# Grouped-query cross-attention layers: all value products of a tile moved behind the tile's last row-maximum products

## What is computed

```python
# 16 query heads, 4 key and value heads, head width 32, n_rep = 4
xn = rmsnorm(x, norm_w)
q = (xn @ wq).reshape(B, T, N_HEADS, HEAD_DIM)
k = (cond @ wk).reshape(B, S, N_KV_HEADS, HEAD_DIM)
v = (cond @ wv).reshape(B, S, N_KV_HEADS, HEAD_DIM)
qg = q.reshape(B, T, N_KV_HEADS, n_rep, HEAD_DIM)
scores = jnp.einsum('btgrd,bsgd->bgrts', qg, k) * scale
attn = jax.nn.softmax(scores, axis=-1)
out = jnp.einsum('bgrts,bsgd->btgrd', attn, v).reshape(B, T, N_HEADS * HEAD_DIM)
return x + out @ wo
```

## Time and profile before

| | |
|---|---|
| Time, median of 3 runs | 4637.84 us (4637.76 to 4638.88) |
| The profiled execution: time | 4637.64 us |
| its span, first to last instruction | 4635.9 us |
| mean granted TensorE clock | 0.976 of full speed |
| PE busy | 4336.0 us, 94% |
| DVE busy | 2565.3 us, 55% |
| ACT busy | 1986.6 us, 43% |
| POOL busy | 1809.3 us, 39% |
| a1's loop, by the repeated pattern | about 2471 to 4620 us of the span |

### The profile page before, as it was taken

How to read it: one execution, slowest core, us unless ns; L and a number is a source line. 1 busy time by engine, 2 the same in 40 slices (tenths; PEclk the granted TensorE clock), 3 DMA queues, 4 the chain that set the end, 5 groups by cost and what they waited for, 6 DMA issues and landing times. The chain is left out here.

```text
span 4635.9 us, 63591 instructions
## 1 busy us (share of the span) xinstructions
PE 4336.0 (94%) x20066; PEld 2694.6 (58%) x20066; DVE 2565.3 (55%) x3575; ACT 1986.6 (43%) x2444; POOL 1809.3 (39%) x923
## 2 busy tenths in 40 slices
PE   7999799996999999999978999999999998999998
PEld 6888588883556555655644554544554554455454
DVE  2122200014555455545447777787777777777776
ACT  2111211112333333333325566566656656666665
POOL 0000000002353444344434556555555555555655
PEclk9999899997999999999988999999999999999999
DMA  4333422224444444444442223322322322232233
GB/s 155 130 127 131 155 80 82 79 88 131 107 115 115 109 102 120 115 109 113 107 125 62 81 73 90 88 83 81 92 81 75 94 84 86 82 88 79 77 95 97
DMA packets 301729, 461.95 MB, mean 100 GB/s; under 512 B 44955, under 2 KB 95131, under 8 KB 301693
## 3 DMA queue, kind: packets, MB, share of 16 engines
q1 hardware_dynamic: 301692, 461.50, 34.4%
HBM read 227.88 MB, written 102.76 MB: 71 GB/s over the span
## 5 line engine op out<-in xcount | busy, mean ns | idle before, releaser
L813 DVE TENSOR_REDUCE a_max_cols<-a_ps 128x1 f32<-128x512 f32 x2072 | 1323.4, 677 | 329.4 <-PE a_ps L937 327.0
L707 ACT ACTIVATE a_probs<-a_ps 128x1024 f32<-128x1024 f32 x1024 | 1018.6, 1027 | 735.8 <-PE a_ps L958 732.7
L937 PE MATMUL a_ps<-a_k_ops,a_q_ops 96*128 96x512 f32 (+1 forms) x2592 | 955.0, 433 | 42.7 <-DVE a_max_cols L813 30.9
L937 PEld LDWEIGHTS a_ps<-a_k_ops,a_q_ops 96*128 96x128 f32 (+1 forms) x2592 | 459.8, 190 | 627.0 <-DVE a_max_cols L813 490.9
L958 PE MATMUL a_ps<-a_q_ops,a_k_ops 128*128 128x512 f32 x2560 | 780.0, 407 | 36.3 <-ACT a_probs L707 20.7
L595 POOL TENSOR_TENSOR a_probs<-a_probs 128x1024 f32<-128x1024 f32 x192 | 463.3, 2413 | 726.9 <-PE a_ps L974 705.7
L974 PE MATMUL a_ps<-a_probs,a_v 128*32 128x512 f32 (+1 forms) x4096 | 674.6, 610 | 0.0
L958 PEld LDWEIGHTS a_ps<-a_q_ops,a_k_ops 128*128 128x128 f32 x2560 | 462.5, 190 | 215.7 <-ACT a_probs L707 104.4
L595 POOL TENSOR_TENSOR a_sums<-a_probs 128x1024 f32<-128x1024 f32 x192 | 454.3, 2385 | 5.0 <-ACT a_probs L707 5.0
L595 POOL TENSOR_TENSOR a_sums<-a_sums,a_probs 128x1024 f32<-128x1024 f32 x192 | 455.2, 2390 | 0.3
L601 POOL TENSOR_TENSOR a_qn_lo<-a_qf,a_qn_hi 128x512 fp32r<-128x512 f32 x99 | 126.7, 1280 | 791.2 <-ACT a_qn_hi L662 791.2
(11 more groups left out here) (92 smaller groups left out, 5615.5 us busy)
## 6 DMA issues: line engine op xcount, KB each, us to landing
a_k_ops<-k_scratch SPq DMA_DIRECT2D x201, 256.0 KB, 4.0
a_q_ops<-a_qn_hi SPq DMA_DIRECT2D x792, 64.0 KB, 2.0
k_scratch<-kp_out SPq DMA_DIRECT2D x88, 512.0 KB, 2.8
a_q_ops<-a_qn_hi SPq DMA_DIRECT2D x268, 128.0 KB, 2.3
a_x_raw<-out_t SPq DMA_DIRECT2D x26, 1024.0 KB, 5.3
a_q_ops<-a_qn_lo SPq DMA_DIRECT2D x396, 64.0 KB, 2.0
a_x_res<-out_t SPq DMA_DIRECT2D x96, 256.0 KB, 3.1
out_t<-a_results SPq DMA_DIRECT2D x96, 256.0 KB, 2.0
```

What stands on the lines that cost most here:

```text
L707: act.activation(probs[:, s], ps[:, 2 * (s % 2):2 * (s % 2) + 2, :], ACT.Exp)\
L813: dve.tensor_reduce(max_cols[:, col:col + 1], bank(MAXB[n]), AX.X, ALU.max, negate=True).then_inc(reduced, 1)
L937: last = pe.matmul(bank(MAXB[n]), q_ops[0:rows(p), s, h, p, q * P:(q + 1) * P], k_ops[0:rows(p), s, k_head(h), p, :], start=(p == 0), stop ...
```

## The change

Only PE's order in a1 is changed. The four output groups leave the loop over r and stand behind it, directly ahead of the denominators, so that six groups of the same form follow one another. The wait for `ms_step`, which in t0 stood ahead of the first output group, moves with it into `outputs`. For a0 the new table gives the same order as before. No instruction is added or removed.

```diff
-    OUT_AT = (2, 3, 5, NS - 1) if has_norm else (1, 2, 3)
+
+    OUT_AT = {} if has_norm else {1: (0,), 2: (1,), 3: (2,)}
+    OUT_LAST = [kt for kt in range(KT) if not any(kt in kts for kts in OUT_AT.values())]
...
                     pe.wait_ge(normed, 1 + it * T + t)
+                    if has_norm and t == 0:
+                        pe.wait_ge(ms_step, MS * (it + 1) + 1)
...
                     for r in range(NS):
-                        if has_norm and r == NS - 1:
-                            outputs(it, t, KT - 1)
...
-                        if r in OUT_AT and not (r == NS - 1 and has_norm):
-                            if has_norm and t == 0 and r == OUT_AT[0]:
-                                pe.wait_ge(ms_step, MS * (it + 1) + 1)
-                            outputs(it, t, OUT_AT.index(r))
-                    if not has_norm:
-                        outputs(it, t, KT - 1)
-                    else:
+                        for kt in OUT_AT.get(r, ()):
+                            outputs(it, t, kt)
+                    for kt in OUT_LAST:
+                        outputs(it, t, kt)
+                    if has_norm:
                         denominators(it, t)
```

## The result

The changed kernel takes 4807.85 us (median of 4 runs, 4804.99 to 4811.39) against 4638.11 us before (4 runs, 4637.76 to 4638.88): ratio 1.0366, 95% interval 1.0348 to 1.0384, slower by 170 us. The forecast of 4790 us was 18 us low and the sign was right. The changed kernel's profiled execution took 4811.39 us, with a span of 4809.6 us.

A forecast was written before the change was run, and what follows sets the result against it. It took DVE to set the pace in the loop over r and PE, in line with ACT, the other half. 4637.6 us + 142 for four tiles over 24 iterations + 11 for weight splits = 4790 us, range 4735 to 4850.

The forecast's parts named there:

- The mechanism: Output groups lie in PE time covered by DVE's reductions; moved behind the loop, four cost 3.56 us uncovered per tile.
- three signs of being wrong: Maxima closer than 0.61 us, t0 growing by less than 3 us, or a granted clock in the loop not 1.00.
- The order alone: Sum over four tiles: t0 3.4, t1 0.55, t2 1.17, t3 0.80, so 5.9 us per iteration, 142 us.
- the line of groups: Behind the last maxima: entered after 0.55 us, then four groups at 0.89 us each before the denominators.
- the last maxima: In t0 they stay where they are, the first output group takes the denominators' place, and t0 grows 3.4 us.
- The clock: First rival: it falls in t0's thin loop, 43 us over 24 tiles, 4833; all 96 tiles 4960; beyond t0 0.13.
- the likeliest case: The main case, chance 0.70: 142 us from the four tiles plus 11 us from weight-splitting tiles, 4790 us.
- The x split in t1: DVE splits x under the output groups, projection only 0.4 us later; exposed table load delays t2: t1 +0.55, t2 +0.3.
- The weight-splitting tiles: In three t1 and three t0, two of four groups run at half clock: 1.8 us each, 11 us.
- The groups in the loop cost nothing at all: In t0 DVE never pauses, so moving the groups out of the loop frees nothing there.
- the second rival: PE is the bound and its switches delay DVE; each group saves 0.31 us, 119 us in all, 4519 us; chance 0.05.

The follow-up runs named there:

- dup_t0_old: The order of before in all tiles, with the first output group of t0 issued twice: 4654.05 us, ratio 1.0034.
- only_t23: The changed kernel with t0 and t1 back in the order of before, so only t2 and t3 have the new one: 4658.62 us, ratio 1.0039.
- warm_mid: The changed kernel with six extra matmuls in every tile, each pair ahead of the second maximum of r = 5, 6, 7: 4803.73 us, ratio 1.0360.
- dup_t3_last: The changed kernel with the first output group of t3 issued twice, behind the loop: 4819.78 us, ratio 1.0390.
- only_t0: The changed kernel with t1, t2 and t3 back in the order of before, so t0 alone has the new one: 4758.16 us, ratio 1.0252.
- t1_old: The changed kernel with t1 back in the order of before: 4773.99 us, ratio 1.0283.
- warm_t1: The changed kernel with six extra matmuls in t1, two behind the maxima of each of r = 5, 6 and 7: 4812.53 us, ratio 1.0365.
- only_t0_warm: only_t0 with six extra matmuls in t0, two behind the maxima of each of r = 5, 6 and 7: 4722.43 us, ratio 1.0188.

## Why the prediction was right, and where its terms were off

The mechanism was right: groups that lay beside DVE's reductions now stand in the open, and DVE waits for the denominators instead. That the time came out within 18 us is in part luck: two errors of opposite sign met. Of the forecast's own three signs of being wrong, one came outright: the granted clock in the loop was not 1.00 but 0.85 over t1. One came by a hair, since the maxima ran every 0.60 us and not every 0.61. The third stayed away narrowly: t0 grew by 3.05 us, and less than 3 would have been the sign.

1. **The order alone was over-sized.** Tiles of the changed kernel with no fall of the clock: t0 22.48 (+3.05, forecast 3.4), t1 20.53 in nine iterations (+0.26, forecast 0.55), t2 19.55 (+0.94, forecast 1.17), t3 30.59 (+0.42, forecast 0.80). Together 4.67 us per iteration, 112 us, where I had 5.92 and 142. The four values come from different iterations; no run had the whole new order free of falls. In t2 and t3 the step at fault is the line of groups: entered after 0.43 us, not the 0.55 taken from the earlier trace rows, with groups of 0.865, not 0.89, and reductions every (8.45 - 0.63) / 13 = 0.60 us instead of 0.61. Over four groups and eleven reductions that makes 0.12 + 0.10 + 0.11 = 0.33 us. In t0 the last maxima, which I took to stay where they were, let the groups begin 13.93 us into the tile, where the denominators had begun 14.16 us into it (3740.78 - 3726.85 against 3381.00 - 3366.84). With the 0.10 of the groups and 0.03 of the two behind them this is 0.36 us, the gap between 3.4 and 3.05.
2. **The clock was a rival and should have been in the sum.** I gave it to t0 alone, 0 to 43 us, and kept it out of the likeliest case since no gap comes near 2 us. No iteration of the changed kernel is free of it. In 12 it falls in a t1 without a weight split, where it makes 23.01 of 20.53 (2.48 us), and in seven in such a t0 (24.2 us once, else 25.0 to 25.2, of 22.48). In the tiles without a weight split that adds up to 46 us. In place of a long idle gap the traces show waits for a maximum's bank of 0.8 to 0.9 us in t0, and in t1 one wait of 1.18 us for ACT. The Trainium skill (TensorE: Matmul & The Clock Gate, Why this matters for your kernels) warns of long idle gaps between bursts; the clock fell here without one, and measurement decides.
3. **The x split in t1.** It was right that the late split no longer holds the projection of q (the wait of 1.42 us is gone) and that the table load passes on to t2. In the iteration shown the load ends at 3677.92 and the first exponential of t2 starts at 3677.93, 1.22 us behind the tile's first score product, where that was 0.65 us before. With t1 in its old order t2 is 0.46 us shorter (I had 0.3).
4. **The weight-splitting tiles.** The 11 us that I added for them did come. The six tiles concerned grew by 13 us more than the order alone gives. The largest is the t1 that went from 25.4 to 29.9 us, its granted clock from 0.93 to 0.77. By length alone this is hard to see, since nearly every iteration with such a tile lacks the fall of the clock elsewhere. So the sum is 112 + 13 + 46 = 171 us, where I had 142 + 11 = 153.
5. **"The groups in the loop cost nothing at all"**, said of t0, held for the four that stand there, since moving them out won nothing back. As a reason it was too strong: by dup_t0_old a fifth costs 0.88 us.

That the switches saved would win (the second rival) is refuted for t2 and t3 by only_t23. The Trainium skill (TensorEngine Tiling (Array Packing), Key Properties) has TensorE drain at a change of tiling mode. These traces agree that a change costs time (1.2 to 1.3 us for a group alone, 0.865 in a line), but not by what mechanism. Three more changes in a tile are cheaper than 3.5 us in the open.

What stays open: why the length of an ordinary iteration is 95.6 us in the changed kernel, in warm_mid and in dup_t3_last, which do different amounts of work. The low stretches of the changed kernel are mostly also 95.6 us apart, and what one tile gains another loses to the clock. I take it that the fall's place in the iteration shifts until the two fit, but no run separates this from chance.

## What to carry to other kernels

Work on a nearly full engine may still be free where it stands: ask which engine sets the pace in each stretch, and move work out of a stretch only if it is that engine's. Batching operations of one form saves the switches (some 0.3 us each here) and costs their cover (up to 0.86 us each), so batch as far as the other engine has work queued, and no further. And where a change thins out TensorE's work, put a fall of the clock into the sum; afterwards compare stretches and not only times, since a fall can move to another stage and hide what an edit did.

## What the hardware showed that I had not expected

- The granted clock fell to 0.50 behind stretches in which the profile shows TensorE idle for no more than 1.2 us at a time. Six matmuls per t0 whose results are thrown away took 30 to 36 us off only_t0.
- The falls moved between t0 and t1, from kernel to kernel and within one kernel. Where both tiles are thinned, an edit to one of them did not rid the loop of falls (t1_old, warm_t1); where t0 alone was, it did (only_t0_warm).
- Groups of four matmuls in separate column groups follow each other every 0.86 us at full clock and take 6.05 / 4 = 1.51 us on average across a fall.
